# Attention, layer normalisation and a mixture of experts on one core: tile offsets, scatters under way, and who reads the first norm's statistics

## The reference

```python
x = L0_attn_x                                        # (4, 1024, 512)
qkv = x @ w_qkv                                      # 16 heads of 128
probs = softmax(q @ k.T / sqrt(128))
x = layernorm(x + (probs.T @ v) @ w_o)               # sum over the queries: 'bhqk,bhkd->bhkd'

scores = sigmoid(x @ router_w.T)                     # 32 experts in 8 groups
topk_idx = top 4 experts within the best 3 groups of scores + bias
topk_w = 2.5 * scores[topk_idx] / sum
# each expert takes at most 160 tokens: slots_token, slots_w are filled by dest
Yf = (silu(Xp @ W_gate) * (Xp @ W_up)) @ W_down * slots_w
out = zeros.at[slots_token].add(Yf)
shared = silu(x @ shared_gate.T) * (x @ shared_up.T) @ shared_down.T
x = layernorm(x + out + shared)
```

## Time and profile before

| | us |
|---|---|
| median of 3 runs | 2949.03 |
| lowest, highest | 2943.35, 2951.62 |
| the profiled execution | 2938.12 |
| its span, first to last instruction | 2936.4 |
| PE busy in it | 2813.8 (96%) |
| DVE, ACT, POOL busy | 2196.4, 1362.3, 724.2 |

### The profile page before, as it was taken

The page is one execution under the profiler, slowest core; times in us unless marked ns, Lnnn a source line. Parts: engine busy times, 40 slices in busy tenths (PEclk is TensorE's granted clock), DMA queues, the critical chain, the costliest instruction groups (busy, mean ns, idle before and its releaser), DMA issues.

```text
span 2936.4 us, 42081 instructions
## 1 busy us (share of the span) xinstructions
PE 2813.8 (96%) x13168; PEld 2299.5 (78%) x13168; DVE 2196.4 (75%) x3392; ACT 1362.3 (46%) x2337; POOL 724.2 (25%) x655
## 2 busy tenths in 40 slices
PE   8999999999999999999999999999998968799998
PEld 6788888877888888788888887888877757688876
DVE  5888888898888888888888898888887635333346
ACT  4555555555554555555545555555443111144434
POOL 2112121211221111112121211222211445466610
PEclk9999999999999999999999999999998878899999
DMA  3111111112111111211111112111102301288843
GB/s 112 36 37 32 36 32 39 36 61 75 33 36 39 32 32 34 102 36 32 36 36 32 39 53 84 36 32 36 40 25 73 101 15 37 82 235 240 246 145 131
DMA packets 216792, 192.82 MB, mean 66 GB/s; under 512 B 18748, under 2 KB 170380, under 8 KB 216704
## 3 DMA queue, kind: packets, MB, share of 16 engines
q1 hardware_dynamic: 202368, 180.55, 19.4%
q0 software_dynamic: 14336, 11.23, 2.1%
HBM read 165.80 MB, written 35.82 MB: 69 GB/s over the span
## 4 chain that ended last, share of the span: by engine, by line
PE 86%; DVE 6%; issue 5%; DMA 1%; ACT 1%; another core or an unknown queue 0%; POOL 0%; SPq 0%; DVEq 0%; POOLq 0%; ACTq 0%
PE banks L1626 34%; PE banks L1641 23%; PE banks L1664 12%; PE banks L1599 5%; PE banks L1551 4%; PE banks L1612 3%; PE banks L1560 2%; PE banks L1651 2%; DVE neg_max L1190 1%; DVE colsum L1205 1%; PE banks L1586 1%; PE banks L1493 1%; DMA slot_table<-entry,slot 0%; DVE qk L1212 0%
## 5 line engine op out<-in xcount | busy, mean ns | idle before, releaser
L1626 PE MATMUL banks<-xt,w_sb 128*128 (+1 forms) x4608 | 1139.2, 396 | 9.7 <-DVE xt L1288 9.7
L1626 PEld LDWEIGHTS banks<-xt,w_sb 128*128 128x128 f32 x4608 | 867.6, 188 | 217.1 <-DVE xt L1288 10.3
L851 ACT ACTIVATE rows_a<-banks,neg_max 128x1024 f32<-128x1024 f32 x512 | 572.6, 1118 | 960.2 <-DVE neg_max L1190 960.2
L1190 DVE TENSOR_REDUCE neg_max<-banks 128x1 f32<-128x1024 f32 x512 | 625.6, 1222 | 324.0 <-PE banks L1641 323.7
L1641 PE MATMUL banks<-qk 128*128 128x512 f32 x3072 | 791.8, 393 | 2.6 <-ACT rows_a L851 2.6
L1641 PEld LDWEIGHTS banks<-qk 128*128 128x128 f32 x3072 | 578.4, 188 | 135.1 <-issue 3.4
L1205 DVE SCALAR_TENSOR_TENSOR colsum<-rows_a,inv,colsum 128x1024 f32<-128x1024 f32 x448 | 585.9, 1308 | 17.9
L607 POOL TENSOR_TENSOR w_sb<-raws,w_sb 128x512 fp32r<-128x512 f32 x192 | 256.1, 1334 | 1292.5 <-ACT w_sb L805 1292.5
L1664 PE MATMUL banks<-wo_sb,val 128*128 128x512 f32 x1536 | 376.7, 394 | 12.8 <-DVE y_sb L1240 12.8
L1664 PEld LDWEIGHTS banks<-wo_sb,val 128*128 128x128 f32 x1536 | 288.0, 189 | 82.6 <-DVE y_sb L1240 18.8
L612 POOL TENSOR_TENSOR wo_sb<-wo_raw,wo_sb 128x512 fp32r<-128x512 f32 x64 | 91.9, 1437 | 431.3 <-ACT wo_sb L811 431.3
(11 more groups left out here) (164 smaller groups left out, 2259.3 us busy)
## 6 DMA issues: line engine op xcount, KB each, us to landing
raws<-in_w_qkv SPq DMA_DIRECT2D x192, 256.0 KB, 2.9
wo_raw<-in_w_o SPq DMA_DIRECT2D x64, 256.0 KB, 2.8
y_sb<-in_x SPq DMA_DIRECT2D x32, 256.0 KB, 3.7
raw_own<-in_w_gate SPq DMA_DIRECT2D x16, 512.0 KB, 4.9
raw_own<-in_w_up SPq DMA_DIRECT2D x16, 512.0 KB
raw_own<-in_w_down SPq DMA_DIRECT2D x16, 512.0 KB
raws<-in_xT SPq DMA_DIRECT2D x25, 256.0 KB, 2.9
x_rows<-y_sb SPq DMA_DIRECT2D x24, 256.0 KB, 3.6
```

Source lines behind the costliest of these rows:

```text
L851: act.activation(ex[:, t % 2], p_s[:, t % 2], ACT.Exp, bias=neg_max[:, t % 2], accum_out=rowsum[:, t % 2]).then_inc(act_e, 1)
L1190: dve.tensor_reduce(neg_max[:, t % 2], p_s[:, t % 2], AX_X, ALU.max, negate=True)\
L1626: ins = pe.matmul(p_g[:, g % 2], w_sb[:, a, r, c], xt_part(batch_par, b, c, half * NB, NB), start=(c == 0 and (a, b) == PASSES[0]), stop=( ...
```

## The change

1. **Tiles.** A tile `aligned` of 104 floats (416 bytes) that nothing reads or writes stands behind `n_shift`. `mv` (32 bytes) goes, and `n_mean` and `n_square` (32 bytes each) come. Everything behind `n_shift` lies 448 bytes further on; 149568 + 448 is 293 × 512.
2. **Scatters.** `UNDER_WAY` is 2 in place of 3.
3. **First norm.** ACT reads each tile twice: Identity with scale −1/D and an accumulated sum, which is the negative mean, then Square with that as its bias and an accumulated sum. Its own output goes to unused space. DVE's `bn_stats` and `bn_aggr` go; `scale_x` waits for ACT (`act_q`) and multiplies the sum by 1/D in `ln_rsqrt`.
4. **Last pair.** ACT's `hi_t(0, ·)` stand ahead of the exponential of t = 0 and 2, DVE's `lo_t(0, ·)` at t = 0 and 2 in place of 1 and 3, and `gate_up(0, 0)` gives 6 matmuls at t = 4 and 5 in place of 3, 4 and 5.
5. **After attention.** `norm(6)` and `norm(7)` are taken apart and moved: `scale_x(6)` stands before `weigh(0)`, `scale_x(7)` behind the third share's sums. ACT's reads and writes of these chunks, and SP's `store_x(7)`, move with them.

```diff
@@ ln_rsqrt @@
-    link.step(dve.tensor_scalar(v, var, eps, None, ALU.add))
+    link.step(dve.tensor_scalar(v, var, times, eps, ALU.mult, ALU.add))
@@ tiles @@
-    UNDER_WAY = 3
+    UNDER_WAY = 2
-    mv = sb("mv", [P, TT, 2])
+    n_mean = sb("n_mean", [P, 2, TT])
+    n_square = sb("n_square", [P, 2, TT])
+    aligned = sb("aligned", [P, 104])
@@ SP @@
+        sp.wait_ge(act_q, 2 * TT * 6)
         load_rows(0)
...
         store_x(6)
-        store_x(7)
...
         load_rows(4)
+        store_x(7)
         sp.wait_ge(pe_t, TT * 4)
         load_rows(5)
@@ ACT @@
+        def read_x(c, tiles=range(TT)):
+            for j in tiles:
+                rows = y_sb[:, (c % 2) * TT + j]
+                on_act.wait_ge(dve_y, T * (PB * (c // 2 + 1) - 1) + (c % 2) * TT + j + 1)
+                on_act.wait_ge(dve_st, c - 1)
+                on_act.wait_ge(act_q, 2 * (TT * c + j))
+                unused = rows_c[:, 0] if c < 6 else exT[:].rearrange("p q k s -> p (q k s)")[:, 0:D]
+                act.activation(unused, rows, ACT.Identity, scale=-1.0 / D,
+                               accum_out=n_mean[:, c % 2, j:j + 1]).then_inc(act_q, 1)
+                on_act.wait_ge(act_q, 2 * (TT * c + j) + 1)
+                act.activation(unused, rows, ACT.Square, bias=n_mean[:, c % 2, j:j + 1],
+                               accum_out=n_square[:, c % 2, j:j + 1]).then_inc(act_q, 1)
...
-                    exp_tile(n, t)
-                    if t >= 6 and finished(i, s) is not None:
-                        write_x(finished(i, s), range(2 * t - 12, 2 * t - 10))
                     if is_last(i) and s == 1 and t in (0, 2):
                         hi_t(0, t)
                         hi_t(0, t + 1)
+                    exp_tile(n, t)
+                    if 1 <= t <= TT and finished(i, s) is not None:
+                        read_x(finished(i, s), [t - 1])
+                    if t >= 6 and finished(i, s) is not None:
+                        write_x(finished(i, s), range(2 * t - 12, 2 * t - 10))
...
+        read_x(6, range(0, 2))
         sigmoid(0, 3)
...
-        write_x(6)
+        sigmoid_r(0)
...
-        sigmoid_r(0)
...
-        write_x(7)
+        read_x(6, range(2, 4))
...
         sigmoid_r(1)
+        write_x(6)
...
+            if u == 2:
+                read_x(7)
             hidden(n, 2)
...
+            if u == 2:
+                write_x(7)
@@ DVE @@
-        def read_x(c, j):
-            if j == 0:
-                on_dve.wait_ge(dve_y, TT * (c + 1))
-            link.then(dve.bn_stats(bn[:, j], y_sb[:, (c % 2) * TT + j]))
         def scale_x(c):
-            link.settle_idle(spare[:])
-            for j in range(TT):
-                link.then(dve.bn_aggr(mv[:, j], bn[:, j]))
-            link.settle()
+            on_dve.wait_ge(act_q, 2 * TT * (c + 1))
             on_dve.wait_ge(act_ln, TT * (c - 1))
-            ln_rsqrt(dve, link, EPS, mv[:, :, 1], small[:, 0], n_scale[:, c % 2], small[:, 2])
-            stt(out=n_shift[:, c % 2], in0=mv[:, :, 0], scalar=-1.0, in1=n_scale[:, c % 2],
-                op0=ALU.mult, op1=ALU.mult).then_inc(dve_st, 1)
+            ln_rsqrt(dve, link, EPS, n_square[:, c % 2], small[:, 0], n_scale[:, c % 2], small[:, 2], 1.0 / D)
+            tt(n_shift[:, c % 2], n_mean[:, c % 2], n_scale[:, c % 2], ALU.mult).then_inc(dve_st, 1)
...
-                    if is_last(i) and s == 1 and t in (1, 3):
-                        lo_t(0, t - 1)
+                    if is_last(i) and s == 1 and t in (0, 2):
                         lo_t(0, t)
+                        lo_t(0, t + 1)
...
-        norm(6)
...
-        norm(7)
...
+        scale_x(6)
         weigh(0)
...
+            if u == 2:
+                scale_x(7)
@@ PE @@
-                    if is_last(i) and s == 1 and 3 <= t <= 5:
-                        gate_up(0, 0, range(6 * (t - 3), 6 * (t - 2)))
+                    if is_last(i) and s == 1 and t in (4, 5):
+                        gate_up(0, 0, range(6 * (t - 4), 6 * (t - 3)))
-        gate_up(0, 0, range(18, 24))
+        gate_up(0, 0, range(12, 24))
```

More of the change, by code:

```diff
@@ L55, with ln_rsqrt @@
 NEWTON = 3
-def ln_rsqrt(dve, link, eps, var, v, g, a):
-    link.step(dve.tensor_scalar(v, var, eps, None, ALU.add))
+def ln_rsqrt(dve, link, eps, var, v, g, a, times=1.0):
+    link.step(dve.tensor_scalar(v, var, times, eps, ALU.mult, ALU.add))
     link.step(dve.tensor_scalar(a.bitcast(U32), v.bitcast(U32), 1, None, ALU.logical_shift_right))
@@ L311, in layer @@
     ro_c, ln_c = sem("ro_c"), sem("ln_c")
-    dve_st, act_ln = sem("dve_st"), sem("act_ln")
+    act_q, dve_st, act_ln = sem("act_q"), sem("dve_st"), sem("act_ln")
     pe_t, act_t, dve_t = sem("pe_t"), sem("act_t"), sem("dve_t")
@@ L1018, in _ @@
         link = Chain(dve, ln_c)
-        def read_x(c, j):
-            if j == 0:
-                on_dve.wait_ge(dve_y, TT * (c + 1))
-            link.then(dve.bn_stats(bn[:, j], y_sb[:, (c % 2) * TT + j]))
         def scale_x(c):
-            link.settle_idle(spare[:])
-            for j in range(TT):
-                link.then(dve.bn_aggr(mv[:, j], bn[:, j]))
-            link.settle()
+            on_dve.wait_ge(act_q, 2 * TT * (c + 1))
             on_dve.wait_ge(act_ln, TT * (c - 1))
-            ln_rsqrt(dve, link, EPS, mv[:, :, 1], small[:, 0], n_scale[:, c % 2], small[:, 2])
-            stt(out=n_shift[:, c % 2], in0=mv[:, :, 0], scalar=-1.0, in1=n_scale[:, c % 2],
-                op0=ALU.mult, op1=ALU.mult).then_inc(dve_st, 1)
-        def norm(c):
-            for j in range(TT):
-                read_x(c, j)
-            scale_x(c)
+            ln_rsqrt(dve, link, EPS, n_square[:, c % 2], small[:, 0], n_scale[:, c % 2], small[:, 2], 1.0 / D)
+            tt(n_shift[:, c % 2], n_mean[:, c % 2], n_scale[:, c % 2], ALU.mult).then_inc(dve_st, 1)
         def stats_o(c, tiles=range(TT)):
@@ L1272, in pair @@
                         add_tile(n, t - 1)
-                    if 1 <= t <= 5 and finished(i, s) is not None:
-                        if t <= TT:
-                            read_x(finished(i, s), t - 1)
-                        else:
-                            scale_x(finished(i, s))
-                    if is_last(i) and s == 1 and t in (1, 3):
-                        lo_t(0, t - 1)
+                    if t == 5 and finished(i, s) is not None:
+                        scale_x(finished(i, s))
+                    if is_last(i) and s == 1 and t in (0, 2):
                         lo_t(0, t)
+                        lo_t(0, t + 1)
         dve.memset(ones_f, 1.0).then_inc(dve_1, 1)
```

## The result

The changed kernel takes 2856.47 us (median of 4 runs, 2854.75 to 2861.37) against 2946.19 before (2939.88 to 2951.62, 4 runs). The ratio is 0.9699, 95% interval 0.9674 to 0.9724: 3.0% faster. The forecast was 2905 with a range from 2870 to 2946, so the direction was right and the size was not.

A forecast was written before the change was run, and what follows sets the result against it. PE's back-to-back matmuls, busy 96% of the span, were taken to bound the kernel. Terms −39 − 2 − 3 − 10 − 1 + 3 + 8 = −44 took 2949 to 2905 us, range 2870 to 2946.

The forecast's parts named there:

- Strip: Attention: like offsets for all tiles bring a head from 34.26 to about 33.6 us, net −39.
- something left behind: L1641 in attention: each unlike-offset group seems to slow the next; without this, 48 × 4.7 ns saves 0.23 us a head.
- Statistics on ACT: Batch boundaries in attention: moving norm statistics from DVE to ACT saves 0.5 us at six chunks, −3 (−13 to +6).
- The sign that was named: Second boundary chunk: PE's waits near 2.9 us would show that moving the statistics worked.
- Last pair: Last pair of heads: earlier DVE steps shorten two PE waits, 3.9 + 3.7 + about 2.4 of half clock, −10.
- Late load: SP's queue: store_x(7) ahead of the load of turn 5's rows makes that load late, +3 (0 to +7).
- Scatters: POOL's routing: two under way take 1.4 us each, +0.13; sum +8, range −25 to +15.
- first train: First train of scatters: landings of 4 to 5 us make it about 5 us longer with two under way.
- the standstill: ACT idle 31.64 us until 2371, DVE and PE too; unexplained, taken to end with the first three scatter trains.
- The second rival: Routing: like offsets work and the standstill of 2340 to 2371 goes, −78, 2871 us; chance 0.15.
- The prediction's own sign of being wrong: Wrong if a head still takes 34.26 us, or the routing phase gets shorter by more than 10 us.
- Landings stretch: Rival: landings (L) staying at 4.5 us make scatters 2.6 us, 2974 us; decides at L above 3.2; chance 0.04.

The follow-up runs named there:

- e2: Changed kernel with its unused strip 64 bytes longer; ratio 0.988 to the kernel before.
- e13: Changed kernel with its unused strip 128 bytes longer; ratio 0.987 to the kernel before.
- e1: Kernel before with only a strip of 448 unused bytes behind n_shift added; 2895.96 us, ratio 0.985.
- e12: Changed kernel with its unused strip 256 bytes longer; ratio 0.972 to the kernel before.
- e8: Changed kernel with the statistics of chunks 0 to 5 back on DVE; ratio 0.972 to the kernel before.
- e7: Changed kernel with the last pair's steps back in their old order; ratio 0.976 to the kernel before.
- e11: Changed kernel with store_x(7) behind load_rows(5) on SP instead of ahead of it; 2866.73 us, ratio 0.974 to the kernel before.
- e4: Kernel before with two scatters under way and nothing else changed; ratio 0.991.
- e3: Changed kernel with three scatters under way; ratio 0.984 to the kernel before.
- e17: Changed kernel with three scatters under way, a strip 512 bytes longer and one 232-column memset behind each scatter; ratio 0.972 to the kernel before.
- e15: Changed kernel with three scatters under way and two chained memsets behind each, the next scatter not waiting for the last memset; ratio 0.981 to the kernel before.
- e18: Changed kernel with three scatters under way and a 232-column memset behind each, run again beside the changed kernel; 2850.36 us, ratio 0.970 to the kernel before.
- e5: Changed kernel with three scatters under way and one small memset behind each scatter; ratio 0.984 to the kernel before.
- e6: Changed kernel with four scatters under way; ratio 0.984 to the kernel before.

## Why the prediction was right and wrong, step by step

- **Strip: right, in cause and size.** Forecast 33.6 us a head and −39 at attention's end; measured 33.54, 39 to 41 between like and unlike offsets (e2, e13 against the changed kernel), 35 to 38 in the trace of e1, 43 in its median. The unit of 256 in which the offsets were counted is now shown (e12). One clock and one shape gave 232.5 and 226.7 here. The rule in the Trainium skill, "TensorE: Matmul & The Clock Gate", section "Wait — 56ns, not 53.3ns?", by which the warm spacing depends on the columns alone, would have given 0; the trace disagrees, and none of the groups read here has its 215.7 ns. That L1641 and L1664, whose own two operands lie at like offsets before as after, also come down when w_sb is put right was forecast for L1641 as "something left behind"; it happened, and how one group slows the next stays unexplained.
- **Statistics on ACT: right, as far as can be told.** Forecast −3, measured −2 to −5 (e8 and e1 against the others). Two reads of a tile take ACT 1.6 us, as forecast. The aggregation's 0.4 came off the wait for 0.25 to 0.3 of it (e8, e1, e2). The sign that was named, a wait near 2.9, did not show in the changed kernel, since the strip lengthens the same wait by 0.3 (e1), which the forecast left out: 3.44.
- **Last pair: right.** Forecast −10 as 3.9 + 3.7 + 2.4; measured −10.2 in the trace, with 3.9 (5.94 to 2.02) and 3.6 (5.24 to waits of 1.6 together) off the two waits, and 9.5 to 10.6 by e7, of which some 6 reach the end.
- **Late load: happened, but priced on the wrong path.** The wait was 5 to 6 us instead of 3, and taking it away is worth nothing (e11). In the changed kernel POOL waits only 4 us for DVE inside its row of scatters, so a wait of PE has room beside it.
- **Scatters: the step that failed.** Every price of a single scatter held: 1.4 (measured 1.45), first train five later (its first six steps take 16.3 us against 11.0). The step that failed is "it ends with the trains. If it still does, 48 scatters bring +5 + 4": the standstill was kept as it was and the slower scatters were added to it, which made the term +8. "DVE and PE too" was also misread: the earlier trace rows show ACT alone, and PE's timeline above shows that PE still gave single matmuls with gaps up to 2361 and only then waited, for DVE, which waited for ACT. The runs showed that the standstill and the gaps hang on the scatters' spacing: when it grew from 1.27 to 1.45, some 30 us went (e4: 27; e3 and e17 against the changed kernel), so the row of scatters was −23.4 in the trace in place of +14, of which +11 for scatters. The second rival named this outcome, at 0.15 and −25, with the argument against it that 0.3 us of idle POOL show a queue that is not full. That argument was the error: idle time between two scatters on POOL says nothing of what they hold up elsewhere. The rival's own reason, a queue that is emptied more often with two, is not what decides either: three permits at 1.45 do the same (e17). The range was too narrow for the same reason: its low end, 2870, lay at the rival's middle, 2871, and the measured 2856 lies under even the rival's 2862 to 2885. The gaps that could go were 31 us of PE alone, plus waits of 12 and more that hung on them. The prediction's own sign of being wrong, a routing phase shorter by more than 10 us, is what came.
- **A slip in the sum.** Of the 48 scatters six at 2.6 for 1.9 are 4.2, not 5, and 42 at +0.13 are 5.5, not 4: 9.7 together for 9, which changes nothing here.
- **Landings stretch: not by much at two, but the point from which it decides was about right.** Landings made POOL wait 38 us in the row, and it was shorter all the same. The point was put at over 1.9 us a scatter; e15 at 1.87 is just there, 248 us.

What stays open: what the scatters hold up. At 1.27 us spacing PE gives single matmuls that wait for nothing in the program, in steps of 0.7 us, and ACT does not start work whose input is there: its waits ahead of `raws` that the profile ends with "remote" come to 62 us before and 29 to 49 in e1, e3, e5 and e6, and to 0 to 11 in the changed kernel, e4, e17 and e18. At 1.45 both are mostly gone. Neither the number of permits (e17) nor the time that landings take (median 3.2 us before, 3.4 after, of those that the profile gives) tells the two apart. It was not tried whether the size of a scatter or its descriptors matter.

## What to carry to other kernels

Where PE has a steady stream, compare the start-to-start time of groups of one shape: if they differ at one clock, look at the byte offsets of the stationary and the moving tile modulo 256, and try an unused strip that makes them alike. Where engines show "issue" waits in the middle of a group while another engine issues many small indirect DMAs, slow those DMAs a little: 1.27 to 1.45 us each made a row of 128 of them 25 to 40 us shorter. A standstill that the profile shows and you can't explain is the widest term of the sum; give it the full width in both directions.

## What the hardware showed

- Matmuls of 512 columns of fp32r at full clock start every 226.7 ns when stationary and moving tile are at like offsets modulo 256 bytes (e1, e12, the changed kernel), and every 232.5 to 233 when they are 64 or 128 off (before, e2, e13).
- Indirect DMAs at 1.27 us spacing make PE give single matmuls 0.7 us or multiples apart, 31 to 57 us of "issue" waits over 128 of them (before, e1, e3, e5, e6); at 1.45 there are 8 to 11 (e17, e18), at 1.87 none (e15).
- On POOL a second short instruction that waits for the first costs far more than it lasts: two memsets of 0.11 us behind each scatter, the second waiting on a semaphore for the first, widened the spacing from 1.27 to 1.87 (e15), while a single one of 232 columns took 0.30 and made 1.45 (e17).
